# Attention stage of a decoder layer: cross-attention tiles placed inside the self-attention steps of the next batch

## The chip, the cores and the metric

The kernel runs on one core of one Trainium2 chip. The metric is the device time of one execution in microseconds (us); shown are the median, lowest and highest of three runs. A core has five engines that run beside each other, each with its own instruction queue: TensorE (PE) multiplies matrices into PSUM banks, VectorE (DVE), ScalarE (ACT) and GpSimd (POOL) work on tiles elementwise, and SyncE (SP) issues all DMAs here. They wait for each other on semaphores. TensorE's clock is granted at full or half rate; the profile gives its mean in a stretch.

## The reference

One pre-norm decoder layer in fp32: `x += attn(layernorm(x)); x += cross(layernorm(x)); x += ffn(layernorm(x))`, with x of 4 batches x 512 rows x 1024 columns.

- Self-attention: 32 query heads and 16 key/value heads of 32 columns, query heads h and h + 16 share key/value head h. It is causal, the scores are scaled by 1/sqrt(32), and q, k, v have biases.
- Cross-attention: the queries are the normalised x itself, keys and values are both `ctx_1024` (4 x 64 x 256, 8 key/value heads, 4 query heads for each), with an additive 512 x 64 mask.
- Feed-forward: `silu(x Wg) * (x Wu)`, then `Wd`, with 3584 hidden columns and weights given as 4-bit codes with one scale for 64 weights.

## The kernel before, in words

**Precision.** An fp32 matmul is made of three fp16 ones. Each operand is cut into a high half (rounded to fp16, on ACT) and a low half (the rest), and high x high, high x low and low x high are summed in PSUM. For self-attention scores the three are stacked as 96 rows of one matmul (`q_rows`, `k_rows`; row 96 carries minus the row maximum). SP does this stacking with 12 small DMAs for each of K and the two Qs (`stack_rows`, L278).

**Work units.** A batch has 4 units (`UNITS`) of 4 pairs; a pair is one key/value head with its two query heads. A unit needs four projections ("kinds": K, two Qs, V; `project`, L471), 24 matmuls of 512 columns each, V in 128-column pieces. A pair has 5 chunks of scores (`score`, L501). DVE takes their block maxima (`maxima`, L920), PE turns these (`turn_max`), ACT negates them, SP stacks them (`stack_max`, L290). Then PE computes transposed scores (`t_score`, L523), ACT takes the exponential (`exps`, L731) and the high half (`high_parts`, L738), DVE (chunks 1 and 3) or GpSimd (chunks 0, 2, 4) the low half (L917, L379), and PE weighs the values with 60 small matmuls (`weigh`, L539). DVE divides (`pair_out`, L938) and GpSimd adds into `x_sb` (`add_pair`, L382), which holds all four row tiles of the batch, 512 rows x 1024 columns.

**Order of the work.** Each engine has its program written out by hand. A hardware loop over batches 0 to 2, and batch 3 after it, runs `unit` for g = 0 to 3 and then `tail`. In `unit` the projections of the next unit are put between the chunks of the current pairs. `tail` is the cross-attention: it begins when all pairs have been added to `x_sb`. It has 16 tiles (4 row tiles x 4 groups of 8 heads): PE scores (L564), DVE adds the mask and takes the maximum (`x_soft`, L949), GpSimd subtracts it (`shift`, L391), ACT takes the exponential (L745), PE turns (L591), ACT and DVE cut in halves (L752, L960), PE weighs (L579), DVE divides (L965), GpSimd adds (L397). In the tail PE also does the next batch's first unit of projections and the scores of its first two pairs. Row tiles are then stored by `store_x` to the DRAM tensor `x2` and the next batch's rows loaded into the same place. `feed_forward` (L1087) follows as a second block and reads `x2`.

**Start.** 16 weight pieces are loaded into the space of `x_sb`, and cut by ACT (L691) and DVE (L826), beside the first projections. GpSimd writes the constants (L425 to L452).

Of the kernel before, what the change touches and what calls it, by code (L numbers as in the profile page):

```python
# [8 lines left out]
FP32 = mybir.dt.float32  # L9
# [86 lines left out]
def attention(nc, t, dram):  # L96
# [7 lines left out]
    with ExitStack() as ctx:  # L104
# [9 lines left out]
        x2T_h = sb("x2T_h", [P, 2, CT, P], FP16)  # L114
        x2T_l = sb("x2T_l", [P, 2, CT, P], FP16)
        stats = sb("stats", [P, 2, 2, 6], FP32)
        mean_var = sb("mean_var", [P, 2, 2], FP32)
        var_eps = sb("var_eps", [P, 2], FP32)
        rstd = sb("rstd", [P, 2], FP32)
        xn = sb("xn", [P, 2, C], FP32)  # L120
        proj32 = sb("proj32", [P, 2, HALF], FP32)
        nat_h = sb("nat_h", [P, 3, T], FP16)
        nat_l = sb("nat_l", [P, 3, T], FP16)
        v32 = sb("v32", [P, QT, PAIRS, D], FP32)
# [7 lines left out]
        o32 = sb("o32", [P, 2, QT, 2, D], FP32)  # L132
        k_raw = sb("k_raw", [P, KVX, TC], FP32)
        v_raw = sb("v_raw", [P, KVX, D], FP32)
        s_top = sb("s_top", [P, 2, 8], FP32)

        s32 = p32[:, 0:2, :].rearrange("p s (a t) -> p s a t", t=TC)
        e32 = p32[:, 2:4, :]
        px_h, px_l = p_h[:, 0, 0:2, :], p_l[:, 0, 0:2, :]

        w_raw = x_sb[:, :, :].rearrange("p s (c n) -> p s c n", c=2)
        bank = [ctx.enter_context(nc.psum_tensor(f"bank{i}", [P, HALF], FP32)) for i in range(8)]
        LN_BANK, PROJ_BANK, T_BANK, MAX_BANK, O_BANK = 0, 2, 4, 6, 7
# [4 lines left out]
        w_loaded = [sem(f"w_loaded{i}") for i in range(QT)]  # L148
# [3 lines left out]
        x_loaded = sem("x_loaded")  # L152
        ctx_loaded = sem("ctx_loaded")
        ctx_step = sem("ctx_step")
# [10 lines left out]
        rows_stacked = sem("rows_stacked")  # L165
# [8 lines left out]
        max_stacked = sem("max_stacked")  # L174
# [4 lines left out]
        p_low_v = sem("p_low_v")  # L179
# [16 lines left out]
        stored = sem("stored")  # L196
        dve_tick = sem("dve_tick")
        sp_tick = sem("sp_tick")
        pool_tick = sem("pool_tick")
        block = ctx.enter_context(nc.Block())  # L200

        STACKS = 3 * 3 * 4
        NP = UNITS * PAIRS
        NCH = NP * CHUNKS
        NX = QT * 4
        NW = UNITS * CT // 2
        LATE = NW - 4
        CUTS_BEFORE = (7, 9, 10)
# [3 lines left out]
        def ln_first(b, first):  # L212
            return 0 if first else 8 * b - 4

        def ln_cross(b, last):
            return 8 * b + (4 if last else 8)


        BY_VECTOR = (1, 3)

        def low_cut(b, n):
            pair, k = n // CHUNKS, n % CHUNKS
            by_vector = k in BY_VECTOR
            before = sum((kk in BY_VECTOR) == by_vector for kk in range(k + 1))
            each = len(BY_VECTOR) if by_vector else CHUNKS - len(BY_VECTOR)
            return (p_low_v if by_vector else p_low), each * (NP * b + pair) + before
# [28 lines left out]
        def _(sp):  # L255
            def held(ge_sem, value):
                sp.wait_ge(ge_sem, value)
                sp.sem_inc(sp_tick, 1)

            def load_row(b, i, at, first=False):  # L260
                src = dram["x"][bass.ds(b, 1), P * i:P * i + P, :].rearrange("b p c -> p (b c)")
                if not (first and i < 2):
                    held(ln_turned, 2 * at - 2)
                sp.dma_start(xn[:, i % 2, :], src).then_inc(row_loaded[i % 2], 16)

            def load_x(b, rt):
                src = dram["x"][bass.ds(b, 1), P * rt:P * rt + P, :].rearrange("b p c -> p (b c)")
                sp.dma_start(x_sb[:, rt, :], src).then_inc(x_loaded, 16)

            def load_w(n):  # L270
                g, c = n // 4, 2 * (n % 4)
                if n >= QT:
                    sp.wait_ge(w_low, n - QT + 1)
                sp.dma_start(w_raw[:, n % QT, :, :],
                             dram["w"][c:c + 2, :, HALF * g:HALF * g + HALF].rearrange("c p n -> p c n"))\
                    .then_inc(w_loaded[n % QT], 16)

            def stack_rows(b, g, kind):  # L278
                held(proj_low, 3 * (UNITS * b + g) + kind + 1)
                for j in range(4):  # L280
                    for r in range(3):
                        if kind == 0:
                            src = (nat_h, nat_h, nat_l)[r]
                            dst = t.k_rows[D * r:D * r + D, g % 2, j, :]
                        else:
                            src = (nat_h, nat_l, nat_h)[r]
                            dst = t.q_rows[D * r:D * r + D, g % 2, 2 * j + kind - 1, :]
                        sp.dma_start(dst, src[D * j:D * j + D, kind, :]).then_inc(rows_stacked, 16)

            def stack_max(b, g, half):  # L290
                held(max_out, 2 * (UNITS * b + g) + half + 1)
                sp.dma_start(t.q_rows[96:97, g % 2, PAIRS * half:PAIRS * (half + 1), :]
                             .rearrange("o s (q n) -> o (s q) n", n=P), neg_max[:, half, :])\
                    .then_inc(max_stacked, 16)

            def load_context(b):
                kT = dram["ctx_kT"][bass.ds(b, 1), :, :].rearrange("b d n -> d (b n)")
                v = dram["ctx_v"][bass.ds(b, 1), :, :].rearrange("b t n -> t (b n)")
                for r in range(4):
                    sp.dma_start(k_raw[D * r:D * r + D, :, :].rearrange("p g t -> p (g t)"), kT)\  # L300
                        .then_inc(ctx_loaded, 16)
                for j in range(2):
                    sp.dma_start(v_raw[TC * j:TC * j + TC, :, :].rearrange("p g d -> p (g d)"), v)\
                        .then_inc(ctx_loaded, 16)

            def store_x(b, rt):
                dst = dram["x2"][bass.ds(b, 1), P * rt:P * rt + P, :].rearrange("b p c -> p (b c)")
                held(x_added, NX * b + 4 * (rt + 1))
                sp.dma_start(dst, x_sb[:, rt, :]).then_inc(stored, 16)
                held(stored, 16 * (QT * b + rt + 1))  # L310

            def batch(b, last):
                for g in range(1, UNITS):
                    if g == UNITS - 1 and not last:
                        for i in range(2):
                            load_row(b + 1, i, ln_first(b + 1, False) + i)
                    stack_rows(b, g, 0)
                    stack_rows(b, g, 1)
                    stack_max(b, g - 1, 1)
                    stack_rows(b, g, 2)  # L320
                    stack_max(b, g, 0)
                if not last:
                    for i in range(2, 4):
                        load_row(b + 1, i, ln_first(b + 1, False) + i)
                stack_max(b, UNITS - 1, 1)
                for rt in range(QT):
                    if not last:
                        for kind in range(3 if rt == 0 else 0):
                            stack_rows(b + 1, 0, kind)
                        if rt == 1:  # L330
                            load_context(b + 1)
                        if rt == QT - 1:
                            stack_max(b + 1, 0, 0)
                    store_x(b, rt)
                    if not last:
                        load_x(b + 1, rt)

            sp.wait_ge(zeroed, 1)
            for i in range(2):
                load_row(0, i, i, True)  # L340
            for n in range(4):
                load_w(n)
                if n < 2:
                    load_row(0, 2 + n, 2 + n, True)
# [3 lines left out]
            for n in range(4, LATE):  # L348
                load_w(n)
                if n == LATE - 2:  # L350
                    stack_rows(0, 0, 0)
            stack_rows(0, 0, 1)
            stack_rows(0, 0, 2)
            for n in range(LATE, NW):
                load_w(n)
            stack_max(0, 0, 0)
            load_context(0)
            held(w_low, NW)
            for rt in range(QT):
                load_x(0, rt)  # L360
            with sp.Fori(0, B - 1) as b:
                batch(b, False)
            batch(B - 1, True)

        @block.gpsimd
        def _(pool):
            def held(ge_sem, value):
                pool.wait_ge(ge_sem, value)
                pool.sem_inc(pool_tick, 1)

            def ln_root(at, s):
                held(ln_stat, 4 * at + 4)
                nc.gpsimd.tensor_tensor(rstd[:, s:s + 1], var_eps[:, s:s + 1], t.minus_half[:, :],
                                        ALU.pow).then_inc(ln_rstd, 1)

            def low_parts(b, n):
                held(p_high, NCH * b + n + 1)
# [1201 lines left out]
```

## Time and profile before

| | us |
|---|---|
| median of 3 runs | 3001.11 |
| lowest, highest | 2996.11, 3006.49 |
| the profiled execution | 2988.39 |
| its span in the trace | 2986.6 |
| PE busy in the span | 2664.2 |
| DVE busy | 2153.1 |
| ACT busy | 1576.9 |
| POOL busy | 1098.2 |

The span reaches from the first instruction to the last. Busy time of an engine is the union of its records; a matmul's record is longer than the time to the next one's start, since matmuls are pipelined. A stage is read by cutting the span into windows.

### The profile page before, as it was taken

To read this page: it belongs to the slowest core of one execution; us is meant where nothing else is said; L and a number is where in the kernel's file an instruction comes from. 1 tells how busy PE (TensorE), PEld (TensorE's weight loads), DVE (VectorE), ACT (ScalarE), POOL (GpSimd) and SP (SyncE) were. 2 spreads that over 40 slices of the span, in tenths; PEclk is the share of its full clock that TensorE was granted. 3 is DMA by queue.
4 is the path that set the end of the run, shared out by engine and by line. 5 is a ranking of instruction groups with operands and counts; after the bars stand their busy time and mean duration, and the time that the engine had idled before them with its cause. 6 is when DMAs were issued, how large, how long until landed. Compare 5 with 4: busy or idle time off the path is not lost.

```text
span 2986.6 us, 54660 instructions
## 1 busy us (share of the span) xinstructions
PE 2664.2 (89%) x18464; PEld 1418.8 (48%) x18464; DVE 2153.1 (72%) x3004; ACT 1576.9 (53%) x2794; POOL 1098.2 (37%) x940
## 2 busy tenths in 40 slices
PE   5887787789778861889999999999999999999999
PEld 3555555556556541434444444444444444444444
DVE  5666666666676665798787787877878778697772
ACT  3554456345535534765474554745547465474550
POOL 2333334333443443343242432424324243252430
PEclk8999898899799965899999999999999999999999
DMA  4210211111021005021111111111111111111112
GB/s 163 61 45 20 80 37 32 44 53 45 19 72 41 18 15 173 22 64 52 48 57 43 56 52 47 57 43 56 54 45 57 43 56 54 45 57 43 56 39 112
DMA packets 97872, 162.10 MB, mean 54 GB/s; under 512 B 20720, under 2 KB 39664, under 8 KB 97648
## 3 DMA queue, kind: packets, MB, share of 16 engines
q1 hardware_dynamic: 97648, 159.47, 16.9%
q8 instruction: 97, 1.59, 0.2%
q14 instruction: 127, 1.04, 0.1%
HBM read 123.61 MB, written 16.78 MB: 47 GB/s over the span
## 4 chain that ended last, share of the span: by engine, by line
PE 56%; DVE 2%; ACT 1%; issue 1%; DMA 1%; POOL 0%; DVEq 0%; ACTq 0%; SPq 0%; POOLq 0%
PE f_bank L1334 37%; PE f_down L1354 19%; DMA codes<-in_codes 1%; DVE line L1458 1%; ACT line L1383 0%; DVE f_stats L1472 0%; DVE fT_l L1485 0%; ACT f_xn L1394 0%; ACT fT_h L1402 0%; PE f_down L1316 0%; ACT line L1380 0%; DVE w L1464 0%; DVE h L1494 0%; DVE y L1499 0%; DVE f_mean_var L1475 0%
## 5 line engine op out<-in xcount | busy, mean ns | idle before, releaser
L1458 DVE TENSOR_TENSOR line<-line 128x512 f32<-128x512 f32 x1008 | 916.8, 961 | 41.2 <-issue 30.5
L1383 ACT ACTIVATE line<-codes 128x512 f32<-128x512 int32 x1008 | 589.7, 620 | 384.0 <-DVE line L1458 278.6
L1334 PE MATMUL f_bank<-fT_h,up_h 128*128 128x512 f16 x1792 | 680.9, 380 | 3.7 <-DVE fT_l L1485 2.4
L1334 PE MATMUL f_bank<-fT_l,up_h 128*128 128x512 f16 x1792 | 680.6, 380 | 0.0
L1334 PE MATMUL f_bank<-fT_h,up_l 128*128 128x512 f16 x1792 | 680.4, 380 | 0.0
L1499 DVE SCALAR_TENSOR_TENSOR y<-f_down,y 128x1024 f32<-128x1024 f32 x224 | 274.4, 1225 | 191.0 <-PE f_down L1354 191.0
L379 POOL TENSOR_TENSOR p_l<-p,p_h 128x512 f16<-128x512 f32 x192 | 227.3, 1184 | 431.6 <-ACT p_h L742 430.7
L1354 PE MATMUL f_down<-dn_h,hT_h 128*128 128x512 f16 x896 | 340.7, 380 | 9.0 <-DVE y L1499 9.0
L1259 POOL TENSOR_TENSOR w<-w,scales 128x512 f32<-128x512 f32 x168 | 263.9, 1571 | 217.8 <-DVE w L1464 217.8
L1264 POOL TENSOR_TENSOR up_l<-w,up_h 128x512 f16<-128x512 f32 x112 | 148.2, 1324 | 531.3 <-ACT up_h L1388 531.3
L1354 PE MATMUL f_down<-dn_l,hT_h 128*128 128x512 f16 x896 | 340.6, 380 | 0.0
L1354 PE MATMUL f_down<-dn_h,hT_l 128*128 128x512 f16 x896 | 340.6, 380 | 0.0
L1334 PEld LDWEIGHTS f_bank<-fT_h,up_h 128*128 128x128 f16 x1792 | 175.6, 98 | 215.0 <-DVE fT_l L1485 2.8
L1334 PEld LDWEIGHTS f_bank<-fT_h,up_l 128*128 128x128 f16 x1792 | 175.7, 98 | 212.6 <-issue 1.9
L1334 PEld LDWEIGHTS f_bank<-fT_l,up_h 128*128 128x128 f16 x1792 | 175.7, 98 | 210.6 <-issue 0.8
L924 DVE TENSOR_REDUCE block_max<-bank 128x4 f32<-128x512 f32 x320 | 212.1, 687 | 87.6 <-PE bank L513 87.0
L735 ACT ACTIVATE p<-bank 128x512 f32<-128x512 f32 x320 | 186.1, 597 | 143.3 <-PE bank L535 142.1
L1278 POOL TENSOR_TENSOR hT_l<-h,hT_h 128x512 f16<-128x512 f32 x112 | 173.0, 1544 | 237.3 <-ACT hT_h L1416 237.3
L1380 ACT ACTIVATE line<-codes,above 128x512 f32<-128x512 int32 x168 | 119.9, 714 | 216.0 <-DVE line L1458 178.1
L917 DVE TENSOR_TENSOR p_l<-p,p_h 128x512 f16<-128x512 f32 x128 | 103.8, 811 | 140.4 <-ACT p_h L742 138.7
L1494 DVE SCALAR_TENSOR_TENSOR h<-f_bank,h 128x512 f32<-128x512 f32 x112 | 77.3, 690 | 163.5 <-PE f_bank L1334 156.6
L742 ACT ACTIVATE p_h<-p 128x512 f16<-128x512 f32 x320 | 194.2, 628 | 0.0
(135 smaller groups left out, 4747.0 us busy)
## 6 DMA issues: line engine op xcount, KB each, us to landing
codes<-in_codes SPq DMA_DIRECT2D x168, 256.0 KB, 2.9
scales<-in_scales SPq DMA_DIRECT2D x336, 128.0 KB, 2.9
xn<-in_x SPq DMA_DIRECT2D x16, 512.0 KB, 3.8
x_sb<-in_w SPq DMA_DIRECT2D x16, 512.0 KB, 5.0
q_rows<-nat_h SPq DMA_DIRECT2D x256, 32.0 KB, 1.9
x_sb<-in_x SPq DMA_DIRECT2D x16, 512.0 KB, 3.8
x<-x_sb SPq DMA_DIRECT2D x16, 512.0 KB, 2.6
y<-x SPq DMA_DIRECT2D x4, 2048.0 KB, 12.6
```

The costliest lines, as they stand in the source:

```text
L379: nc.gpsimd.tensor_tensor(p_l[:, dst[0], dst[1], :], p32[:, n % 4, :], p_h[:, dst[0], dst[1], :], ALU.subtract).then_inc(p_low, 1)
L735: nc.scalar.activation(p32[:, n % 4, :], bank[T_BANK + n % 2][:, :], ACT.Exp, scale=SELF_SCALE)\
L742: nc.scalar.activation(p_h[:, n // CHUNKS % 2, n % CHUNKS, :], p32[:, n % 4, :], ACT.Copy)\
L924: nc.vector.reduce_max(block_max[:, n % PAIRS, k, :], bank[LN_BANK + m % 2][:, :].rearrange("p (a n) -> p a n", n=P), AX_X)\
L1259: nc.gpsimd.tensor_tensor(w, w, scales[:, k % 2, :], ALU.mult).then_inc(scaled, 1)
L1264: nc.gpsimd.tensor_tensor(w_l, w32[:, k % 2, :], w_h, ALU.subtract).then_inc(w_low, 1)
L1278: nc.gpsimd.tensor_tensor(hT_l[:, q // NB, cols], h32[:, q % 2, :], hT_h[:, q // NB, cols], ALU.subtract).then_inc(h_low, 1)
L1334: mm = nc.tensor.matmul(bank[(GATE, UP)[kind] + n % 2][:, :], w[:, chunk, kind, P * c:P * c + P], x[:, c, cols], start=(m == 0), stop=(m = ...
L1354: mm = nc.tensor.matmul(down_bank[r % 2][:, half, :], h[:, m // 3, rows], w[:, m // 3, cols], start=(m == 0), stop=(m == 5))
L1383: op = nc.scalar.activation(line[:, m, :], codes[:, slot, :], ACT.Copy, scale=slope, bias=intercept)
L1458: nc.vector.tensor_tensor(line[:, n + 2, :], line[:, n, :], line[:, n + 2, :], ALU.max)\
L1499: nc.vector.scalar_tensor_tensor(y[:, r, :], down_bank[r % 2][:, :, :].rearrange("p a n -> p (a n)"), 1.0 / (H_SCALE * F_SCALE), y[:, r, : ...
```

## The change

1. **Steps.** There are no hardware loops in the attention block. All engines run `step(s)` for s from -6 to 67 (`FROM`, `TO`; GpSimd from 0), where pair s has its transposed scores (offset by three chunks), pair s + 2 its scores, pair s - 1 its weighing and pair s - 2 its division and adding. Each step has 5 slots, one for each chunk. A table `KINDS_AT` and `kinds_in` say which projection runs in which step: one in most, two in the fifth and sixth step of a batch, none in the ninth and tenth, where the next batch's rows are normalised and turned.
2. **Cross-attention.** Tile x of batches 0 to 2 runs in step x + 20 (`X_LAG`), beside the pairs of the next batch, one tile a step: scores in S bank 1 at slot 0, turned into T bank 0 at slot 3, weighed at slot 1 of the next step in a bank of its own. It no longer shares `r_sum`, `o32`, `p32` and `p_h` with the pairs. The tiles of batch 3 run after the last step, in `last_cross`.
3. **x.** In place of `x_sb` (four row tiles) there are `x_unit` (two units of 512 rows x 256 columns, for the pairs) and `x_row` (two row tiles, for the cross tiles). A finished unit is stored to a new DRAM tensor `x1`, and read back by rows; the result of the cross tiles goes to `x2` as before.
4. **Low halves.** All five chunks' low halves of a pair are GpSimd's; DVE does none.
5. **Context.** DVE cuts keys and values in five full-width instructions (before: 13, by blocks), and 12 DMAs lay them out.
6. **Start.** The order of weight cuts, projections and first scores follows the steps; PE waits for all of GpSimd's constants before the first projection. Semaphores for DMAs are split by slot or kind; the `held` ticks are gone.

The core of the diff (the main step functions, and the parts of SP, POOL and PE that the text speaks of):

```diff
-        x_sb = sb("x_sb", [P, QT, C], FP32)
+        x_unit = sb("x_unit", [P, 2, QT, 2, P], FP32)
+        x_row = sb("x_row", [P, 2, C], FP32)
...
+        FROM = -6
+        X_LAG = NP + 4
+        TO = NS + 4
...
+        KINDS_AT = {0: (6,), 1: (7,), 2: (8,), 3: (9,), 4: (10, 11), 5: (12, 13), 6: (14,), 7: (15,)}
...
+        FIRST_STATS = {(7, 1): (0,), (8, 2): (1,), (8, 4): (2,), (9, 2): (3,)}
...
         @block.sync
...
+            def step(s):
+                b, i = divmod(s, NP)
+                follows, crosses = 0 <= b < B - 1, 1 <= b < B
+                u = s // 4 + 1
+                if i == 8 and follows:
+                    load_row(b + 1, 1)
+                if i == 9 and follows:
+                    load_row(b + 1, 3)
+                if s % 2 == 0 and 0 <= s < NS:
+                    stack_max(s // 2)
+                if i % 4 == 0 and u < NU:
+                    stack_rows(u, 0)
+                    stack_rows(u, 1)
+                if i % 4 == 1 and u < NU:
+                    stack_rows(u, 2)
+                if i % 4 == 1 and 2 <= u:
+                    store_x1(u - 2)
+                if i % 4 == 2 and 2 <= u < NU:
+                    load_x(u)
...
+                if i % 4 == 0 and 4 <= s - NP:
+                    x = s - X_LAG - 4
+                    if x >= 0:
+                        store_x2(x // NX, x % NX // 4)
+                if i == 8 and follows:
+                    load_row(b + 1, 2)
+                if crosses and i % 4 == 1:
+                    load_x1(b - 1, i // 4)
...
         @block.gpsimd
...
+            def step(s):
+                x = cross_in(s)
+                for f in (5 * s - 4, 5 * s - 3):
+                    if 0 <= f < CHUNKS * NS:
+                        low_part(f)
+                    if f == 5 * s - 4:
+                        if 2 <= s <= NS + 1:
+                            add_pair(s - 2)
+                        if x is not None:
+                            shift(x, s32[:, x % 2, :])
...
         @block.tensor
...
+            def step(s):
+                x = cross_in(s)
+                kinds = kinds_in(s)
+                pieces = [(q, piece) for q in kinds for piece in range(4)]
+                each = len(kinds)
+                for k in range(CHUNKS):
+                    if 0 <= s + 2 < NS:
+                        score(s + 2, k)
+                    f = 5 * s + k - 3
+                    if 0 <= f < CHUNKS * NS:
+                        t_score(f // CHUNKS, f % CHUNKS)
+                    if k == 0 and x is not None:
...
+                        x_score(x, S_BANK + XS_OF, x2T_h, x2T_l)
+                    if k == 1:
...
+                            x_weigh(y, XO_BANK, px_h, px_l)
...
+                    if k == 3 and x is not None:
...
+                        x_turn(x, T_BANK + XT_OF, s32[:, x % 2, :])
+                    if k == 4 and 1 <= s <= NS:
+                        weigh(s - 1)
+                    for q, piece in pieces[each * k:each * k + each]:
+                        project(q, piece)
```

Of the waits added, three matter for the text: `t_score` of chunk 2 waits for the low part of the cross tile turned in the step before (`x_low`, T bank 0); `stack_rows` and `stack_max` wait in SP's one queue; `ln_stats` of a cross row waits for `x1_loaded`.

## Rows read from the trace of the kernel before

**Rows 1.** Windows by stage: length, busy us of PE, PEld, DVE, ACT, POOL; clock, DMA, GB/s.
```profile
76.00:346.00 270.00, 218.82 (x2584) 149.01 (x2581) 180.20 (x347) 133.51 (x247) 102.36 (x104) 0.92 0.16 49
346.00:640.00 294.00, 240.09 (x2671) 161.60 (x2672) 187.62 (x359) 143.34 (x264) 107.34 (x108) 0.88 0.15 46
640.00:930.00 290.00, 238.61 (x2910) 166.79 (x2909) 190.05 (x370) 146.74 (x272) 114.96 (x115) 0.90 0.15 43
930.00:1062.00 132.00, 109.67 (x1486) 74.17 (x1484) 79.01 (x154) 73.86 (x140) 53.32 (x50) 0.91 0.08 20
1062.00:1142.00 80.00, 45.09 (x384) 35.16 (x384) 54.38 (x108) 23.85 (x40) 30.68 (x37) 0.69 0.07 27
1142.00:2986.60 1844.60, 1769.88 (x8192) 808.36 (x8192) 1420.03 (x1608) 1029.77 (x1801) 672.69 (x502) 0.98 0.18 57
```

**Rows 2.** Timeline of PE: start us, length us, engine, line, operation, count.
```profile
80.07 0.38 PE L490 MATMUL bank<-xT_l,w_h 128*128 128x512 f16 x1
80.28 0.38 PE L490 MATMUL bank<-xT_h,w_l 128*128 128x512 f16 x1
...
95.91 0.22 PE L513 MATMUL bank<-mask_qk,ident_b 128*128 128x128 bf16 x1
...
97.62 0.18 PE L560 MATMUL bank<-v_parts,p_l 128*128 128x33 f16 x1
...
265.16 1.04 PE L466 MATMUL bank<-ident,xn 128*128 128x128 f32 x8
...
280.06 0.19 PE L587 MATMUL bank<-vx_h,p_h 128*128 128x66 f16 x1
...
280.43 0.30 PE L594 MATMUL bank<-ident,p 128*128 128x128 f32 x1
```

**Rows 3.** Waits from 76 to 1143 us: total us, times, longest us.
```profile
PEld bank L587 <- DVE p_l L962: 71.4, 43, 3.5
...
PE bank L587 <- DVE o L972: 56.9, 42, 3.2
...
PEld bank L510 <- DVE block_max L924: 54.8, 83, 2.0
```

**Rows 4.** Timeline of DVE in the last tail, two cross tiles that follow each other.
```profile
1127.08 0.69 DVE L954 TENSOR_TENSOR p<-bank,mask_x 128x512 f32<-128x512 f32 x1
...
1130.06 0.68 DVE L954 TENSOR_TENSOR p<-bank,mask_x 128x512 f32<-128x512 f32 x1
```

**Rows 5.** Single lines: duration ns min/median/max; the last two: busy us, mean ns.
```profile
L379 POOL TENSOR_TENSOR p_l<-p,p_h x192: 1153/1159/1547, 82.9 to 1056.7; 128x512 f16<-128x512 f32 x192
...
L917 DVE TENSOR_TENSOR p_l<-p,p_h x128: 675/709/1468, 84.7 to 1056.1; 128x512 f16<-128x512 f32 x128
...
L1259 POOL TENSOR_TENSOR w<-w,scales x168: 1262/1712/1723, 1150.9 to 2906.0; 128x512 f32<-128x512 f32 x168
...
L394 POOL TENSOR_TENSOR p<-p,s_top 128x512 f32<-128x512 f32 x64 | 66.8, 1043 | 145.2 <-DVE s_top L958 145.2
...
L400 POOL TENSOR_TENSOR x_sb<-o,x_sb 128x256 f32<-128x256 f32 x64 | 47.0, 734 | 32.5 <-DVE o L972 27.5
```

**Rows 6.** Timeline of DVE and ACT: two operations merged into one line.
```profile
81.67 1.28 DVE L924 TENSOR_REDUCE block_max<-bank 128x4 f32<-128x512 f32 x2
...
1105.22 1.07 ACT L697 ACTIVATE x2T_h<-bank 128x512 f16<-128x512 f32 x2
```

**Rows 7.** DMA: issue on SP (ns min/median/max); then KB, median us to landing.
```profile
L288 SPq DMA_DIRECT2D q_rows<-nat_h x256: 507/591/1833, 46.3 to 1015.0; - x128
...
DMA to landing us min/median/max: 1.8/1.9/4.6
...
xn<-in_x SPq DMA_DIRECT2D x16, 512.0 KB, 3.8
...
x<-x_sb SPq DMA_DIRECT2D x16, 512.0 KB, 2.6
```

**Rows 8.** Timeline of POOL: the last constants before the steps.
```profile
35.64 0.32 POOL L451 MEMSET vx_h<- 64x8 f16 x2
```

More of the change, by code:

```diff
@@ L215, in ln_cross @@
[L215 to L226, printed above, removed]
+        FROM = -6
+        X_LAG = NP + 4
@@ new lines, in attention, with xn_slot, x1_slot @@
+        for s in range(TO):
+            LN_ORDER += [("first",) + at for k in range(CHUNKS) for at in first_rows(FIRST_TURNS, s, k)]
+            if last_turn(s):
+                LN_ORDER.append(("cross",) + last_turn(s))
+        LN_ORDER += [("cross", B - 1, rt) for rt in range(QT)]
+        LN_AT = {at: n for n, at in enumerate(LN_ORDER)}
+        def xn_slot(what, b, i):
+            if what == "first":
+                return (i + 1) % 2
+            return 0 if b < B - 1 else i % 2
+        def x1_slot(rt):
+            return rt % 2
@@ L255, in _, with load_row @@
         def _(sp):
[L256 to L268, printed above, removed]
+            def load_row(b, i):
+                slot = xn_slot("first", b, i)
+                at = LN_AT["first", b, i]
+                if at >= 2:
+                    users = [n for n in range(at) if xn_slot(*LN_ORDER[n]) == slot]
+                    sp.wait_ge(ln_turned, 2 * users[-1] + 2)
+                sp.dma_start(xn[:, slot, :], dram["x"][b, P * i:P * i + P, :]).then_inc(row_loaded[slot], 16)
@@ L306, in store_x @@
[L306 to L336, printed above, removed]
@@ L365, in _, with ln_root @@
+            for slot in range(2):
+                sp.wait_ge(x2_stored[slot], 16 * 2 * B)
         @block.gpsimd
         def _(pool):
[L367 to L373, printed above, removed]
+            def ln_root(at):
+                pool.wait_ge(ln_stat, 4 * at + 4)
+                nc.gpsimd.tensor_tensor(rstd[:, at % 4:at % 4 + 1], var_eps[:, at % 4:at % 4 + 1], t.minus_half[:, :],
@@ L666, in _ @@
             pe.wait_ge(selected, 1)
             for i in range(4):
[L668 to L670 removed]
+                for half in range(2):
+                    ln_turn(i, half, PROJ_BANK + half)
             pe.wait_ge(selected, 8)
[L672 to L677 removed]
@@ L678, in _ @@
-            with pe.Fori(0, B - 1) as b:
-                for g in range(UNITS):
-                    unit(b, g, False)
-                tail(b, False)
-            for g in range(UNITS):
-                unit(B - 1, g, True)
-            tail(B - 1, True)
+            for s in range(FROM, TO):
+                step(s)
+            last_cross()
         @block.scalar
```

1251 lines of the change are left out of this document (663 added, 588 removed).

## Prediction

> **What bounds the kernel now.** I read the table of stages first [rows 1]. The feed-forward stage is 1844.6 us of the 2986.6 us span with TensorE (PE) busy for 1769.9, and the diff does not touch it. Everything is decided in the first 1142 us. There PE is busy 219 of 270, 240 of 294 and 239 of 290 us in the three looped batches, 110 of 132 in the last batch's self-attention and 45 of 80 in the last cross-attention. "Busy" overstates it, since a short matmul's record is longer than the distance to the next one: 0.38 us for 512 columns where the next starts 0.21 us later. So I count PE's work by start-to-start distances [rows 2]:
>
> - 512 columns 0.215 us, so one projection kind (24 such, or 96 of a quarter of the width) takes 5.2 us, and 16 kinds a batch 83;
> - scores of a pair, both ways: 7168 columns at the same rate, 3.0 us;
> - weighing a pair: 60 matmuls between the last score's start at 95.91 and 97.62, 1.5 us without that score;
> - a normalised row turned: 8 in a record of 1.04, so 0.9 us;
> - a cross tile: scores of 6 x 256 columns 0.65, turn as half a row 0.44, weighing 0.37 (12 from 280.06 to 280.43), 1.46 together.
>
> A batch is 83 + 16 x 4.5 + 16 x 1.46 + 8 x 0.9 + some 2 for the maxima = 188 us of PE work at full clock, against a period of 290 to 294. VectorE (DVE) is busy for 188 to 190 of it, no more than PE's work, so neither engine fills the period: handoffs do. The list of waits names them [rows 3]: PE waits for the cross tiles' outputs and low halves (56.9 and 71.4 us) and for block maxima (54.8). The last tail shows this bare: its last tiles come one per 3.0 us [rows 4], and the stage takes 80 us for 27 us of PE work.
>
> **The change, part by part.** Cross-attention leaves the tails and runs 20 steps later beside pairs. I work out the time of each kind of step, in which one pair passes through.
>
> *Engine work in a step.* DVE loses the two low parts of a pair (128 x 0.81 = 104 us in all). POOL gains 128 x 1.16 = 148 us [rows 5]. Independent operations start 0.6 apart on DVE and 0.54 on ACT (two records of 0.6 to 0.69 together take 1.28 and 1.07, [rows 6]). A cross step with one kind then has: PE 5.2 + 4.5 + 1.46 + 0.6 for rows and maxima = 11.8 to 11.9; DVE 5 maxima 3.0, pair out 0.6, cross tile 2.7, kinds 0.9, row maxima 0.5, LayerNorm of 8 rows over 16 steps 2.0 = 9.7; ACT 10 x 0.54 for the pair, 1.1 for the tile, 1.3 for kinds, 0.6 for rows = 8.4; POOL 5 x 1.16 + 0.73 + 1.04 + 0.73 = 8.3 [rows 5]. PE has most.
>
> *The longest loop.* T bank 0 is filled by a cross turn in slot 3 and given back by DVE's low part of that tile. Before that, ACT does an exponential, a high part and the tile's high part (0.54 + 0.54 + 0.60), then DVE 0.69, with four handoffs of some 0.06: 2.6 us after the slot-4 transposed scores. PE has weighing and one score (1.8 us) to do meanwhile, so it stalls 0.8. The loop is 12.2 us at full clock with everything else in it hidden (the exponential for the turn comes 0.4 late and is in the sum). Granted clock was 0.88 to 0.92 in these stages and 0.98 where PE is kept full [rows 1]; I take 0.95, which puts 4% on PE's parts: 12.7 us. Without a cross tile the same walk gives 9.9, with the clock 10.3. Two-kind steps: 15.3 and 18.0. Steps 56 to 63, without kinds, are set by ACT and DVE: 9.6.
>
> *SyncE (SP), where a wait is added.* In every fourth step SP first waits for the row maxima (3.8 us into the step), then issues 0.52 + 36 x 0.59 to 0.61 us of stacking, and the last lands 1.9 us later [rows 7]: 28.1 us after the step began. PE needs it at slot 1 two steps on, after 2P + 2.4. At P = 12.7 this is 27.8, so it just fits; at P = 10.3 PE stalls 4.7, and a unit of four steps takes 45 us. In step 8 of each batch the load of the next batch's third row stands behind 24 stacks (14.6 us) and lands 3.8 us after issue; DVE waits for it in slot 4 with the next pair's maxima, the cross low part and so PE queued behind: the step takes 25 us. Step 9, with 8 us of LayerNorm on DVE, takes 13 to 15.5.
>
> *x through DRAM.* Each cross row's x1 is loaded by SP behind the same stacks and the unit's stores; it lands at about 32 us of the unit, DVE asks at 28.4 and has some 1.5 to 3 us of slack. I put 2 us on each of 11 units, a bit more for the first rows: 25 us. Nothing in this trace does such a round trip; below is 0 (DVE's slack hides it), above 6 us a unit (2.6 for the store to land and 3.8 for the load, [rows 7]), 66 us. I take the lower half, since the first row alone has the store ahead of it. Context layout by DMA: DVE saves 8 copies, some 4 us a batch, in its slack (nothing), and the values land 2.7 us late for the first tile of a batch: 8 us in all.
>
> *Start.* PE now waits for the last GpSimd constant (36.0 us, [rows 8]) before any projection, while the old kernel had its first kind out then. Kinds end at 41.5, 46.7, 51.9; SP stacks from 47 to 69.3, the scores follow at 71.2, and two steps with weight cuts bring step 0 to 85 us. The old loop began at 76. +9.
>
> *Sum.* Step 0 at 85. Steps 0 to 15: 45 + 51 (two kinds twice) + 58 (steps 8 to 11) + 45 = 199. Steps 16 to 19: 45. Steps 20 to 31: 2 x 18.0 + 2.7 + 2 x 12.7 + 26 + 15.5 + 6 x 12.7 = 182. Steps 32 to 47: 50.8 + 182 = 232. Steps 48 to 63: 50.8 + 38.7 + 25.4 + 8 x 9.6 = 192. That is 935, with 25 for x1 and 10 for clock in the steps that I took at full rate: 970. Steps 64 to 67 hold only the rest of a pair and one cross tile each, in one chain of 6.5 us (cross scores 0.65, soft 1.4, shift 1.04, exponential, turn, high and low part 0.6 to 0.7 each, handoffs): 28 with the last pair. The last cross-attention: first soft step 10.8 us in, then 16 x 3.0 as now [rows 4], 10 for its rows and 3 to end: 72, where the old stage took 80. The stage ends at 1070 instead of 1142: **-72 us**. The profiled execution took 2988.4 us around its span of 2986.6, and the median of the runs shown is 3001.1, 12.7 above; the same difference off the median gives 2929, said as **2930**.
>
> The gain comes unevenly: of the stretches of [rows 1], 270 becomes 208, 294 about 237 and 290 about 248, but the last batch with what follows it grows from 132 + 80 = 212 to about 302, since the third batch's cross tiles now lie there.
>
> **A rule of the Trainium skill.** DVE's low parts took 0.68 us at least and 1.47 at most, and GpSimd's multiply of two SBUF tiles is 1.26 to 1.72 in the feed-forward stage, its p_l only 1.16 [rows 5]. The Trainium skill ("SBUF — State Buffer", section "Who interferes with whom") says that a DVE instruction with two SBUF inputs contends with a GpSimd instruction that reads SBUF, and the one that comes second is fully blocked. The trace agrees in that both spread upward where they run together. By the rule the move leaves few such DVE instructions, so GpSimd stays at 1.16; were they at the 1.72 of the multiply, a step would cost it 2.8 us more, 11.1, still under 12.7.
>
> **Rivals.**
>
> *All handoffs hidden.* Clean pacing at 11.9 us and rows in time: 0.8 x 40 + 25 = 57 less, 2872. For it: each engine but PE has 3 to 4 us of slack in a cross step. Against: every PE bank still has one owner at a time, and a batch now takes 290 us for 188 of PE work, 1.5 times, while the forecast's cross step asks for 1.07 times.
>
> *SP sets the pace.* Issues of 1.65 to 1.8 us and landings of 4.6 exist already [rows 7], and now eight transfers in 512-byte runs and a row join each unit. At 3 us more for the first half of 15 units: +45, 2975.
>
> *Slower: the T bank held until DVE's low part.* DVE serves pairs, cross tiles and LayerNorm in one written order; if it reaches the low part one soft-step and one maximum late (2 x 0.69 + 0.61 + handoffs, 2.6 us with the step it pushes), each of the 44 steps from 20 to 63 costs 15.3 instead of 12.7: +114, 3043. It turns the sign when such steps exceed 12.7 + 72/44 = 14.3 us. For it: this very release is in the waits now (71.4 us, [rows 3]). Against: DVE has 9.7 us of work in 12.7.
>
> *The change doesn't do what it says* would show as cross tiles still outside the pair steps; the written order excludes it but for the last batch.
>
> **How the numbers follow.** Forecast 0.45 (own range 2895 to 2972), all hidden 0.17, SP 0.18, slower 0.20. A difference under 0.3% (9 us) can't be told from none here. Faster: 0.44 + 0.17 + 0.13 = 0.74; same, from the edges of the last two: 0.08; slower 0.18. The range reaches from a little under the best case to where half of the slower rival is left out: 2860 to 3025.
>
> **What would show it.** PE's stall before slot-0 transposed scores, put down to the cross low part, about 0.8 us a step (2.5 or more would be the slower rival). Step 8 twice as long as its neighbours, with DVE waiting for a row of x. PE waits on stacked q rows of 4 to 5 us a unit in batch 0 and about none later. Attention ending at 1070, feed-forward unchanged at 1845. The mechanism is wrong if cross steps are set by GpSimd, or if the first 20 steps are not the faster ones; the sum is wrong if the mean step from 20 to 47 is over 14.3.

## The result, and the profile after

| | before | after |
|---|---|---|
| median, us (5 runs each) | 2996.11 | 3026.79 |
| lowest to highest | 2990.74 to 3006.49 | 3024.87 to 3032.24 |
| span of the profiled execution | 2986.6 | 3023.5 |

The changed kernel is slower: ratio 1.0103, 95% interval 1.0077 to 1.0128. The forecast was 2930, with a range up to 3025.

The table of stages of the changed kernel, to be laid beside [rows 1]; the columns are the same. The borders of the middle rows are the beginnings of steps 16, 32, 48 and 64, about 1.5 us before GpSimd adds the pair of two steps earlier.

```profile
0.00:84.00 84.00, 44.60 (x253) 24.98 (x254) 45.44 (x55) 27.22 (x34) 15.57 (x26) 0.91 0.44 146
84.00:307.50 223.50, 181.73 (x2151) 122.06 (x2149) 109.31 (x206) 106.69 (x199) 99.67 (x94) 0.89 0.19 52
307.50:574.00 266.50, 206.22 (x2477) 143.15 (x2476) 149.16 (x286) 126.62 (x238) 130.23 (x128) 0.89 0.20 58
574.00:842.00 268.00, 210.55 (x2566) 148.81 (x2565) 156.41 (x305) 128.54 (x243) 135.54 (x136) 0.90 0.22 61
842.00:1069.50 227.50, 177.47 (x2290) 125.96 (x2288) 128.97 (x257) 119.24 (x228) 133.20 (x133) 0.86 0.20 55
1069.50:1178.00 108.50, 54.70 (x544) 42.68 (x542) 66.86 (x132) 31.11 (x53) 44.08 (x54) 0.72 0.17 58
1178.00:3023.50 1845.50, 1767.65 (x8192) 807.00 (x8192) 1423.07 (x1608) 1030.34 (x1801) 667.42 (x502) 0.98 0.18 57
```

Feed-forward is as long as before (1845.5 against 1844.6). Attention ends at 1178 instead of 1142. A batch in the middle takes 268 us instead of 290 to 294, so the steps do gain, some 25 us a batch, but the last batch with what follows takes 336 where it took 212. The forecast's sums for steps 16 to 31, 32 to 47 and 48 to 63 were 227, 232 and 192, with some 12 us each of the 35 that it spread over them; measured are 266.5, 268 and 227.5, so each is 24 to 28 us longer.

How long a step is can be read from GpSimd's pair adds, one a step. Here are those of pairs 25 to 29 in the timeline of POOL:

```profile
500.88 0.73 POOL L519 TENSOR_TENSOR x_unit<-o,x_unit 128x256 f32<-128x256 f32 x1
514.40 0.73 POOL L519 TENSOR_TENSOR x_unit<-o,x_unit 128x256 f32<-128x256 f32 x1
527.22 0.73 POOL L519 TENSOR_TENSOR x_unit<-o,x_unit 128x256 f32<-128x256 f32 x1
540.69 0.72 POOL L519 TENSOR_TENSOR x_unit<-o,x_unit 128x256 f32<-128x256 f32 x1 [0.31 <-DVE o L1098]
559.80 0.72 POOL L519 TENSOR_TENSOR x_unit<-o,x_unit 128x256 f32<-128x256 f32 x1
```

Three ordinary cross steps (one projection kind, one cross tile) take 13.5, 12.8 and 13.5 us (forecast 12.7), and then comes one of 19.1. By the same adds there are eight of this kind, 17 to 21.5 us long where an ordinary step of the same stretch has 10 or 13: the third steps of the eight units whose first two steps hold neither two kinds nor the next batch's rows. What PE waits for is in the brackets of its own timeline; these are long ones of batches 1 and 2, in order of time:

```profile
391.86 0.21 PE L759 MATMUL bank<-vx_h,px_h 128*128 128x66 f16 x1 [6.62 <-DMA vx_l<-v_cut]
...
467.41 0.29 PE L702 MATMUL bank<-q_rows,k_rows 97*128 97x128 f16 x1 [13.13 <-DVE px_l L1113]
...
543.77 0.61 PE L673 MATMUL bank<-k_rows,q_rows 96*128 96x512 f16 x1 [4.10 <-DMA q_rows<-nat_h]
...
603.35 0.39 PE L673 MATMUL bank<-k_rows,q_rows 96*128 96x512 f16 x1 [3.50 <-DMA q_rows<-nat_h]
...
610.87 0.39 PE L702 MATMUL bank<-q_rows,k_rows 97*128 97x512 f16 x1 [0.99 <-DMA q_rows<-neg_max]
...
615.77 0.19 PE L725 MATMUL bank<-v_parts,p_h 128*128 128x33 f16 x1 [1.93 <-POOL p_l L510]
```

The 13.13 is put down to DVE's cross low part (`px_l`), and this is where a releaser misleads: DVE was held in front of it by the third row of the next batch. The list of waits from 80 to 1180 us has the cause in a line of its own, beside the other DMAs (total us, times, longest):

```profile
PEld bank L702 <- DVE px_l L1113: 61.8, 35, 13.7
...
PE bank L673 <- DMA q_rows<-nat_h: 34.5, 9, 5.6
DVE stats L1014 <- DMA xn<-in_x: 34.3, 3, 11.6
...
DVE stats L1014 <- DMA x_row<-x: 29.6, 6, 6.4
...
PE bank L759 <- DMA vx_l<-v_cut: 18.0, 3, 6.6
```

Before, DVE waited 4.4 us for such rows in the whole kernel, and PE 4.8 us for stacked rows after the start. All four DMA waits go back to one queue, SP's. Its timeline around step 32, which PE began at 570.67 (its first score), and around the late row of step 24:

```profile
459.46 0.58 SPq L363 DMA_DIRECT2D x<-x_row  x1
460.09 1.26 SPq L334 DMA_DIRECT2D xn<-in_x  x2
```

```profile
575.61 0.58 SPq L391 DMA_DIRECT2D q_rows<-neg_max  x1
577.28 1.20 SPq L386 DMA_DIRECT2D k_rows<-nat_h  x2
...
592.63 0.59 SPq L386 DMA_DIRECT2D q_rows<-nat_h  x1
593.27 0.58 SPq L363 DMA_DIRECT2D x<-x_row  x1
593.90 1.12 SPq L386 DMA_DIRECT2D q_rows<-nat_h  x1
...
601.40 0.59 SPq L386 DMA_DIRECT2D q_rows<-nat_h  x1
602.03 2.60 SPq L350 DMA_DIRECT2D x<-x_unit  x4
607.39 0.33 SPq L358 DMA_DIRECT2D x_row<-x  x1
607.76 0.58 SPq L391 DMA_DIRECT2D q_rows<-neg_max  x1
```

SP issues without a break from 577.3 to 604.6. The last stack lands near 603.3, when PE goes on; PE had been ready at 599.85 (603.35 less 3.50).

### The profile page after: what moved, and what is told of

It reads as the page before. It is cut to its first block, busy times and chain, and to the rows that moved or that the text cites. A ratio compares the mean times of both kernels' runs of the same rounds, so it can differ in the third digit from the quotient of the medians.

```text
span 3023.5 us, 52802 instructions
## 1 busy us (share of the span) xinstructions
PE 2642.9 (87%) x18464; PEld 1414.6 (47%) x18464; DVE 2079.2 (69%) x2844; ACT 1569.8 (52%) x2794; POOL 1225.7 (41%) x1068
## 4 chain that ended last, share of the span: by engine, by line
PE 56%; DVE 2%; issue 1%; ACT 1%; DMA 1%; POOL 0%; SPq 0%; DVEq 0%; ACTq 0%; POOLq 0%
PE f_bank L1462 36%; PE f_down L1482 19%; DVE line L1586 1%; DMA codes<-in_codes 1%; DVE f_stats L1600 0%; DVE fT_l L1613 0%; ACT line L1511 0%; ACT f_xn L1522 0%; ACT fT_h L1530 0%; PE f_down L1444 0%; DVE w L1592 0%; ACT line L1508 0%; DVE h L1622 0%; DVE y L1627 0%; DVE f_mean_var L1603 0%
## 5 line engine op out<-in xcount | busy, mean ns | idle before, releaser
L1586 DVE TENSOR_TENSOR line<-line 128x512 f32<-128x512 f32 x1008 | 928.8, 972 | 43.7 <-issue 29.1
L510 POOL TENSOR_TENSOR p_l<-p,p_h 128x512 f16<-128x512 f32 x320 | 372.0, 1172 | 452.6 <-ACT p_h L920 451.6
L1074 DVE TENSOR_REDUCE block_max<-bank 128x4 f32<-128x512 f32 x320 | 218.7, 686 | 273.2 <-PE bank L675 270.5
L673 PE MATMUL bank<-k_rows,q_rows 96*128 96x512 f16 (+3 forms) x512 | 143.5, 319 | 79.3 <-DMA q_rows<-nat_h 45.5
L702 PE MATMUL bank<-q_rows,k_rows 97*128 97x512 f16 (+3 forms) x512 | 143.8, 319 | 57.7 <-DVE px_l L1113 49.5
## 6 DMA issues: line engine op xcount, KB each, us to landing
y<-x SPq DMA_DIRECT2D x4, 2048.0 KB, 12.8
```

Of the source, the lines that this page charges most:

```text
L510: nc.gpsimd.tensor_tensor(p_l[:, n % 2, k, :], p32[:, f % 4, :], p_h[:, n % 2, k, :], ALU.subtract).then_inc(p_low, 1)
L1074: nc.vector.reduce_max(block_max[:, n % PAIRS, k, :], bank[S_BANK + S_OF[k]][:, :].rearrange("p (a n) -> p a n", n=P), AX_X)\
L1586: nc.vector.tensor_tensor(line[:, n + 2, :], line[:, n, :], line[:, n + 2, :], ALU.max)\
```

## The experiments

Each ratio is to the kernel before, timed beside it (medians of 2993.5 to 2996.2). The main theory is that order and number of issues on SP make the change slow; the main rival is the prediction's own, the T bank that a cross tile holds. Each text below names its theories anew.

**1. The row ahead of the stacks.**

```diff
                 if s % 2 == 0 and 0 <= s < NS:
                     stack_max(s // 2)
+                if i == 8 and follows:
+                    load_row(b + 1, 2)
                 if i % 4 == 0 and u < NU:
...
-                if i == 8 and follows:
-                    load_row(b + 1, 2)
```

> One edit to the changed kernel: in step 8 of a batch SP issues the load of the next batch's third row ahead of the 24 stacking DMAs instead of behind them. Theory A (queue order on SP: three stalls of 12.4, 13.1 and 12.8 us stand in PE's timeline in front of the first score or transposed score after step 8, each put down to DVE, which waited for this row): each shrinks to under 2 us, 30 to 38 us less than the changed kernel's 3027, so 2990 to 2997. Theory B (the steps are bound by the handoffs of the cross tile, and a stall removed in one place is taken up by the next): 0 to 10 us less, 3017 to 3027, and steps 8 and 9 together still take some 45 us.

Measured 2997.25, ratio to before 1.0009 (0.9997 to 1.002), so 30 us less than the changed kernel. Three stalls of 13 us are gone, and with them the long entries in PE's wait for the cross low part, whose longest is now 2.1 us:

```profile
PEld bank L702 <- DVE px_l L1113: 38.7, 36, 2.1
```

This one misplaced DMA, three times, is as large as the whole loss. It also shows that the 13.13 above was not the T bank's doing.

**2. Half as many query stacks.**

```diff
+            def stack_queries(u):
+                sp.wait_ge(proj_low, 3 * u + 3)
+                for j in range(4):
+                    for r in range(3):
+                        sp.dma_start(t.q_rows[D * r:D * r + D, u % 2, 2 * j:2 * j + 2, :],
+                                     (nat_h, nat_l, nat_h)[r][D * j:D * j + D, 1:3, :]).then_inc(rows_stacked[1], 16)
...
                     stack_rows(u, 0)
-                    stack_rows(u, 1)
...
-                    stack_rows(u, 2)
+                    stack_queries(u)
```

> One edit to the changed kernel: the two query kinds of a unit are stacked by 12 DMAs of two rows' length each in place of 24, so SP issues 24 stacks a unit instead of 36. Theory A (SP's issue time sets when PE may begin the third step of a unit; PE's waits for stacked query rows are 4 to 6 us each, 74.6 us with weight loads counted in, some 45 to 50 us of path): the waits fall to under 1.5 us, the third steps of a unit go from 19 to 21 us to about 14, 35 to 55 us less: 2972 to 2992. It helps the row of step 8 too, which stands behind 12 stacks instead of 24 (7.6 us earlier, at most 20 us of the three stalls), so up to 70 us less is within A. Theory B: under 10 us less. Theory C (the cost lies in moving the bytes, not in issuing: the same bytes take as long): same time as now, with landing times of these DMAs doubled.

Measured 2946.43, ratio 0.9844 (0.9823 to 0.9864): 80 us less than the changed kernel, more than A's 70. The DMAs move twice the bytes each and land as fast, so theory C falls:

```profile
q_rows<-nat_h SPq DMA_DIRECT2D x128, 64.0 KB, 2.0
k_rows<-nat_h SPq DMA_DIRECT2D x128, 32.0 KB, 1.9
```

So it is the number of issues, not the bytes. By the pair adds of both kernels, summed over units of four steps, the time comes from these places: the three units with neither cross tiles nor two kinds (0, 12 and 16) 15 us; the units of the late row (8, 24 and 40), which now stands behind 12 stacks, 19; the two-kind units with the cross values (20, 36 and 52), behind 12 stacks as well, 23; the start and the two-kind unit 4 together 6; and the five cross units that A was about 15, of which 7 in unit 56, which has no kinds, and only 1 to 3 in each of the other four. In these PE still waits about 4 us:

```profile
499.45 0.59 PE L680 MATMUL bank<-k_rows,q_rows 96*128 96x512 f16 x1 [4.26 <-issue]
```

The trace names no releaser, but the last query stack goes out at 497.37 and lands 2 us later, just then. The merged queries must wait for the third kind's low half (the first goes out at 489.56, 6 us into its step) and all come in at once. So the wait has moved from the second chunk of the third step to its first one: by the pair adds the third step falls to 14 or 15 us, and the step before it grows from 13 to 17. A's "waits under 1.5 us" did not come.

**3. The cross tile turned into another bank.**

```diff
-                x = cross_in(n)
-                if k == 2 and x is not None:
-                    pe.wait_ge(x_low, x + 1)
-                else:
-                    free = (CHUNKS * (n - 1) + 4, ...)[k]
+                free = (CHUNKS * (n - 1) + 4, ...)[k]
...
-                        x_turn(x, T_BANK + XT_OF, s32[:, x % 2, :])
+                        if x >= 1:
+                            pe.wait_ge(x_read, x)
+                        x_turn(x, XO_BANK, s32[:, x % 2, :])
```

(ACT's high part and DVE's low part read the same bank.)

> One edit to the changed kernel: the exponentials of a cross tile are turned into the bank that later takes its weighed values, not into T bank 0, so the transposed scores of chunk 2 wait no more for the tile's low half. Theory A (this wait costs what the prediction put on it, 0.8 us of 12.7 in an ordinary cross step, a little more as measured, 13.1): 44 steps x 0.8 to 1.2 = 35 to 50 us less, if nothing else takes its place; 2977 to 2992. In step 8 the wait for the row stays and goes to the score's S bank instead. Theory B (the rival of the prediction, this bank is what made the change slow): 80 us or more less, under 2950. Theory C (ACT's and DVE's order holds PE one slot later anyway): under 10 us less.

Measured 3024.86, ratio 1.0116 (1.0095 to 1.0136): 2 us less than the changed kernel, which can't be told from none. Neither A's 35 to 50 nor the rival's 80. The wait is gone and an ordinary cross step is 0.8 us shorter by the pair adds (12.0 and 12.7 instead of 12.8 and 13.5), but the time is paid elsewhere: PE waits 8 us more for stacked queries and 9 more for the values, and 17.1 us in all for the outputs of the tile before, which lie in the bank now shared. The late rows hold it as before, now at the score's bank; the second line is step 40.

```profile
663.20 0.21 PE L755 MATMUL bank<-vx_h,px_h 128*128 128x66 f16 x1 [9.36 <-DMA vx_l<-v_cut]
...
738.43 0.61 PE L673 MATMUL bank<-k_rows,q_rows 96*128 96x512 f16 x1 [12.65 <-DVE block_max L1068]
```

The values' wait was 6.5 us at this place and is 9.4: PE came earlier and waited longer for an unchanged queue.

**4. All four** (1, 2, 3 and the values' layout ahead of the stacks).

> The three edits above together, and a fourth: the four DMAs that lay out the cross values go ahead of the stacks in the fifth step of a batch (PE waits 6.6, 6.5 and 4.9 us for them now). Theory A says that these are separate places and their gains add but for the part of the row's stall that merging already takes: 35 + 45 + 40 + 15 less some 15 = 120, so about 2905 (2885 to 2935), below the kernel before (2996). Theory B: they share one loop, so the sum is at most 50 us less, above 2975.

Measured 2900.65, ratio 0.9693 (0.9676 to 0.9711): 126 us less than the changed kernel and 3.1% less than before. Attention ends at 1052. By themselves they gave 30, 80, 2 and, for the values (experiment 9), 18: 130. But 2 already takes about 20 of 1 and most of 9, so the three SP edits should give some 90 together, and experiment 7 shows that the rest is the turn bank. Not all SP stalls are gone. PE's wait for the stacks of queries is still there in front of the third step of eight units:

```profile
PE bank L680 <- issue: 36.5, 8, 5.8
```

In the changed kernel the same places hold 45.6 us (34.5 put down to the stacks, 11.1 to nothing).

**5 and 8. The low halves of chunks 1 and 3 back on VectorE**, in the changed kernel and in that with all four edits.

```diff
+                    if k in BY_VECTOR and 0 <= 5 * (s - 1) + k < CHUNKS * NS:
+                        low_part(5 * (s - 1) + k)
```

> One part of the change undone: in the changed kernel the low halves of chunks 1 and 3 are VectorE's again, as before; GpSimd keeps three of five. Theory A (the part costs nothing, since SP's queue sets the long steps and GpSimd was never late): within 10 us of the changed kernel's 3027. Theory B (the part helps: VectorE would be the late one): 10 to 40 us slower, up to 3065. Theory C (the part hurts: DVE's nat_l took 1.23 us at the median against 0.69 before, since it now meets a busier GpSimd, and weighing waited 15 to 21 us for GpSimd's low halves): 10 to 30 us faster, 2997 to 3017, with nat_l back near 0.7 to 1.0 us.

> All four edits and, besides, chunks 1 and 3 of the low halves on VectorE again. With the SP stalls gone the engines' work matters more. Theory A: VectorE has 9.7 us of work in 12.5 us steps and 1.2 more fits, within 8 us of 2901. Theory B (VectorE becomes the bound): 2915 or more. Theory C (GpSimd held it up): 2893 or less.

Measured 3024.25 (ratio 1.0116, 1.009 to 1.0142) and 2906.06 (0.972, 0.9695 to 0.9744): no difference in the first, and 5 us more in the second, less than the intervals tell apart. So the part costs nothing in the steps, as forecast.

**6. The merged queries in the kernel before.**

> The kernel before with the one edit that took 80 us off the changed kernel: both query kinds of a unit stacked by 12 DMAs. Theory A (the long stacking queue only hurts where pairs come in equal steps; the old order has room, PE waited 16.8 us for stacked rows in all, 12 of it at the start): 0 to 15 us less than 2996. Theory B (the old kernel profits as much, so that the change itself is worth nothing): 50 us or more less, under 2946. The edit also makes the second query kind wait for the third, so a small loss up to 15 us is possible under A.

Measured 2988.31, ratio 0.9985 (0.9967 to 1.0002): 5 us less, not told from none. The same edit was worth 80 in the steps. There was little to gain: PE waited only 4.8 us for stacked rows after the start.

**7. All but the turn bank.**

> The row early, the queries merged and the values early, but the cross tile is turned into T bank 0 as in the changed kernel. Beside the run with all four (2900.7) this gives what the turn bank is worth once the SP stalls are gone; alone it was worth 2 us. Theory A (its 0.8 to 1.8 us a step only shows where nothing else is late): 20 to 35 us more, 2920 to 2936. Theory B (it is worth nothing in any setting, the gain of the four came from the other three): within 6 us of 2901.

Measured 2934.76, ratio 0.9817 (0.9792 to 0.9842): the three SP edits give 92 us, and the kernel is 34 us slower than with the turn bank. So the T bank's wait is worth 34 us once these SP stalls are shorter or gone, and 2 us in the changed kernel. PE's waits for the cross low part of this kernel:

```profile
PE bank L709 <- DVE px_l L1120: 26.5, 31, 1.8
```

**9. The values' layout ahead of the stacks, alone.**

> The changed kernel with one edit: in the fifth step of batches 1 to 3, the four DMAs that lay out the cross values go ahead of the unit's stacks. PE waits 6.6, 6.5 and 4.9 us for them in the changed kernel. Theory A (separate place): 12 to 18 us less than 3027, 3009 to 3015. Theory B (the sixth step has two kinds and some slack behind it, and the stacks now start 2.6 us later): 0 to 8 us less.

Measured 3008.53, ratio 1.005 (1.0033 to 1.0067): 18 us less, for waits of 18.0 us, as in theory A.

**10. All low halves on GpSimd in the kernel before.**

```diff
-        BY_VECTOR = (1, 3)
+        BY_VECTOR = ()
```

> The kernel before with one part of the change: all five low halves of a pair on GpSimd, none on VectorE. Theory A (neither engine was late there): within 9 us of 2993. Theory B (in the old units VectorE's wait for ACT's high half, 139 us in all, held up the maxima behind it, and its waits go): 10 to 30 us less. Theory C (GpSimd's chain of 1.16 us each delays weighing): 10 to 30 us more.

Measured 2964.43, ratio 0.9906 (0.9877 to 0.9935): 30 us less, at the edge of B. The prediction had not seen this. In the old units DVE stood 139 us waiting for ACT's high halves with maxima queued behind, and these waits are gone; PE's wait for row maxima falls from 28.0 us to 12.3, and the scores' weight loads wait at most 1.1 us for a block maximum where it was 2.0:

```profile
PE bank L519 <- DVE row_max L934: 12.3, 8, 2.0
```

**11. All four, with x1 stored and read back ahead of the query stacks.**

> The kernel with all four edits and one more: in the second step of a unit SP stores the finished unit and reads the cross row back before it stacks the queries, in the gap in which it waits for the third kind's low half. VectorE waits only 3.6 us for these rows in the kernel with all four. If x through DRAM still costs, 5 to 12 us less than 2901; if it is hidden by now, within 4 us; if the gap is too short for 3 us of issues, the stacks are late: 5 to 20 us more.

Measured 2909.07, ratio 0.9717 (0.9688 to 0.9746): 8 us more by the medians, though the intervals of this run and of experiment 4 overlap. The trace points to a gap on SP that is too short: PE's unnamed waits at the scores (36.5 us in experiment 4) are 47.4. No gain shows, so the way of x through DRAM was hidden by then (DVE waits 3.6 us for it in experiment 4).

**12. The kernel before with 6 and 10.**

> The kernel before with its two cheap edits together: all low halves on GpSimd (2964 alone) and the merged query stacks (2988 alone, before 2994). It gives the fair mark for the equal steps: what the old order reaches with the same small parts. If they add: 2956 to 2964, so that the steps with all four edits (2901) are worth 55 to 63 us by themselves. If SP's queue becomes late in the faster old units, merging helps more there: 2940 to 2955. If the later second query kind now hurts: 2965 or more.

Measured 2960.24, ratio 0.989 (0.9853 to 0.9928): they add. Against this mark the steps with all four edits are 60 us faster.

## Why the prediction was wrong

**The step that failed** is "*SyncE (SP), where a wait is added* ... At P = 12.7 this is 27.8, so it just fits". It fits in none of the four units where it was to fit (28, 32, 44 and 48). At step 32 the first stack goes out 6.6 us after the step began, not 4.3: maxima come at 4.9 and not 3.8, and the K stack then waits for the last transposed scores of the unit whose rows it overwrites, a wait that I left out. Issues start 0.634 apart, not 0.607. `store_x2` (0.63) and two longer issues fall between them. The last lands 32.7 us in, not 28.1. PE is ready at 29.2 instead of 27.8, and the stall is 3.5; in the other three units it is 4.1 to 4.8. The fifth cross unit, 56, runs without kinds: by the prediction's own formula its pace of 9.6 leaves PE ready at 21.6 and stalled for 6.5, but the sum has 8 x 9.6 and no stall. Measured there is 5.6, after 2.1 at the chunk before. What follows from a stall was left out too: the maxima's DMA behind `load_x1` (0.99) and weighing behind GpSimd (1.93) come late after it. For these five units, where the sum had no stall, the third steps cost 6 to 10 us more than ordinary ones, some 35 us together.

The same queue was under-priced in the units where the forecast did see a stall. In units 0, 12 and 16 PE stands 6 to 7 us (3 at the third step's first chunk, which waits for the 24th stack, and 4 at the second) where 4.7 were forecast. The values and the late rows are below.

**The sum by parts**, in us; the units are those of four steps, by the pair adds. The forecast's 35 us for x1 and the clock were spread over all steps.

| part | forecast | measured |
|---|---|---|
| up to step 0 | 85 | 91 |
| steps 0 to 15 | 199 | 216.5 |
| unit 16 | 45 | 56 |
| units 20, 36, 52: two kinds twice, values | 192 | 223 |
| units 24, 40: late row | 134 | 149 |
| units 28, 32, 44, 48: ordinary | 203 | 238 |
| steps 56 to 63, without kinds | 77 | 95 |
| x1 and clock, spread | 35 | in the rows above |
| after step 63 | 100 | 108.5 |
| end of attention | 1070 | 1178 |

So the miss has no single place. The mean step from 20 to 47 is 17.1 us. The prediction's sign for a wrong sum was 14.3, but its own sum has (182 + 232) / 28 = 14.8 there, so this sign could not have told.

I had named the rival "SP sets the pace" at 0.18 and priced it at 45 us. The three edits of SP's order and number alone gave back 92, to 2934.8, and turned a loss against the kernel before into a gain. This is near the miss of 97 us, but it isn't the same time: some 60 of SP's stalls were in the forecast already (14 for step 8, 27 for steps 24 and 40, 11 for units 0, 12 and 16, 8 for the values). Without them it would have said about 2870. That 2934.8 lies near 2930 is chance.

**What else was off, by the terms of the sum.**
- Values late for the first tile of a batch: 2.7 us forecast, 6.6, 6.5 and 4.9 measured; 18 us instead of 8, and experiment 9 gave back 18.
- Steps 24 and 40: 26 forecast, 31 and 30 measured by the pair adds. The cause was named rightly, and its removal gave 30 us.
- Ordinary cross steps are 12.8 us, or 13.5 with a turn of row maxima, forecast 12.7 at a clock of 0.95. The granted clock isn't why: it is 0.99 to 1.00 in such steps, so the forecast's 12.2 at full clock is 0.6 to 1.3 short. The T bank's 0.8 in it was right: with the turn bank such steps take 12.0 and 12.7, and PE is then busy for 11.58 of 12.0. PE's own work was put too low, at 11.8 to 11.9.
- Start: step 0 begins at about 91, forecast 85; DVE's weight cuts stand in front of the maxima (waits of 2.08 and 2.50 us of PE).
- After step 63: 108.5 us, forecast 100.

**The clock** falls in and after the long stalls. The columns are those of the table of stages; the first row lies in ordinary steps, the second in step 30 with the stall, and the third behind it:

```profile
512.00:525.00 13.00, 11.96 (x144) 7.80 (x141) 8.01 (x15) 7.80 (x16) 8.06 (x8) 1.00 0.12 30
...
538.50:557.50 19.00, 12.92 (x135) 7.74 (x134) 11.19 (x22) 6.52 (x14) 9.84 (x9) 0.90 0.33 98
557.50:570.60 13.10, 13.01 (x138) 8.39 (x137) 7.64 (x14) 8.29 (x16) 7.01 (x8) 0.89 0.00 1
```

**What was right.** Feed-forward unchanged; the uneven gain, with the last batch growing (to 336 us, forecast 302); two-kind steps; the step without kinds at about 10; low halves on GpSimd free in the steps; PE the longest engine and not GpSimd. The prediction held against its slower rival that DVE has room, and that holds: the T bank is not what made the change slow (experiments 1 and 3), and its price of 0.8 us in each of 44 steps, 35 us, is what experiment 7 measures, 34. But this price shows only where the stalls on SP leave room for it.

**How the time hid.** Experiments 3 and 7 explain why adding up PE's waits doesn't tell what an edit brings. With the turn bank PE came to the next DMA earlier and stood there longer (9.36 us for 6.5 at the values of batch 2), and only with the three SP edits did the shorter steps count.

What stays open is the wait of 3 to 6 us in front of the third steps, 36.5 us in all, which is left in the kernel with all four edits and which no run took away: that the failed step costs some 35 us in the changed kernel is read from its trace, and no run isolates it. Open is also whether x through DRAM cost anything in the changed kernel (29.6 us of DVE's waits): only the kernel with all four edits was tried, where it was hidden. What the lower clock behind the stalls costs was not measured apart.

## What to carry to other kernels

When work is evened out over steps, count the issues on each DMA queue for the half of the cycle in which they must land, not over the whole cycle, with every wait ahead of the first one: here SP issues for some 30 of a unit's 60 us and is still late. Look in its order for a load that one engine waits for behind many that nobody waits for yet. An edit that takes away a wait on a loop with a second, fixed wait can show nothing until that one is shorter or gone, so try them together before dropping one; and try each part of a large change in the old kernel, where one of them was worth 1%.

## What the runs showed of the hardware

- One DMA from SBUF to SBUF of 64 KB (32 partitions of 2 KB) lands in 2.0 us, one of 32 KB in 1.9 (experiment 2), and both cost SP 0.63 us from start to start. Merging two halved their cost on the queue.
- A VectorE subtraction of two SBUF tiles takes nearly twice its time where GpSimd's low half is already running. `nat_l` after the change, ns min/median/max:

```profile
L1054 DVE TENSOR_TENSOR nat_l<-proj,nat_h x48: 681/1231/1472, 42.8 to 964.5; 128x512 f16<-128x512 f32 x48
```

Before it was 681/693/693 for the same 48. The timelines of both engines show why (the first line is GpSimd's, the second VectorE's):

```profile
103.41 1.16 POOL L510 TENSOR_TENSOR p_l<-p,p_h 128x512 f16<-128x512 f32 x1 [0.24 <-ACT p_h L920]
103.88 1.23 DVE L1054 TENSOR_TENSOR nat_l<-proj,nat_h 128x512 f16<-128x512 f32 x1 [1.33 <-ACT nat_h L890]
```

`nat_l` ends 0.54 us after `p_l` does. So do all 43 that begin inside a `p_l`: the longest, 1.47, begins with 0.92 of it still to run. The five that meet no GpSimd instruction take 0.69. With chunks 1 and 3 back on VectorE (experiment 5) the median is still 1229, since a `p_l` runs at that place of the step there too. In the old kernel with all low halves on GpSimd the median stays at 693. The other way round, in the kernel before, `nat_l` begins at 148.89 and keeps its 0.68, and GpSimd's add of 0.73 us, begun 0.26 later, takes 1.00. The rule of the Trainium skill that the prediction cites ("SBUF — State Buffer", "Who interferes with whom") fits both: the one that comes second is held until the first is done. The prediction looked for its effect on GpSimd; here it fell on VectorE, 26 us in all. Whether any of it is on the path was not tested.
